# Attention plus eight experts on one core: spilled expert weights leave in six pieces over five tiles and come back one piece at a time

## Reference, cut down

```python
x = x + tanh(g_xattn[0]) * xattn(ctx_1024, layernorm(x), mask, ...)   # 32 batches, 8 heads
h = layernorm(x)                                                      # 3584 tokens of 256
conf = sigmoid(h @ conf_w.T + conf_b) * wealth
top_bids, selected = top_k(conf, 2)                                   # 2 of 8 experts per token
...
ffn = (silu(h @ gate_w.T) * (h @ up_w.T)) @ down_w.T                  # 256 -> 1024 -> 256
out = x + tanh(g_ffn[0]) * sum over the two chosen experts, weighted by softmax(top_bids)
```

## Time and profile before

| | |
|---|---|
| median of 3 runs | 1436.77 us (1435.43 to 1438.32) |
| the profiled execution's own time | 1435.85 us |
| its span, first to last instruction | 1434.3 us |
| mean granted TensorE clock | 0.989 |
| busy: PE, PEld, DVE, ACT, POOL | 94%, 68%, 71%, 65%, 34% |
| bytes moved by DMA | 109.26 MB, mean 76 GB/s |

### The profile page before, as it was taken

One profiled execution on the slowest core, in us unless ns is written; L12 is line 12 of the kernel. 1 busy time (PEld: TensorE's weight loads), 2 busy tenths in 40 slices (PEclk: granted clock), 3 DMA queues, 4 the chain that ended last, 5 costly groups with the idle time before them and its releaser, 6 DMA issues.

```text
span 1434.3 us, 41525 instructions
## 1 busy us (share of the span) xinstructions
PE 1351.1 (94%) x13880; PEld 969.2 (68%) x13880; DVE 1023.5 (71%) x2528; ACT 934.8 (65%) x1932; POOL 488.2 (34%) x659
## 2 busy tenths in 40 slices
PE   2999999999999999999999979999999999999996
PEld 1466666666666666666665657688878778887784
DVE  4688888888888888888888776566556654444442
ACT  5687878787787878878787765566656663333331
POOL 4423322433433334334333143433344333222221
PEclk9999999999999999999999979999999999999998
DMA  4010101111111111111112146433376753112461
GB/s 119 27 42 26 42 23 29 52 40 49 34 53 30 41 46 39 49 33 53 31 33 96 41 129 196 107 98 93 98 211 178 228 152 94 31 31 35 120 203 16
DMA packets 56913, 109.26 MB, mean 76 GB/s; under 512 B 10832, under 2 KB 34768, under 8 KB 56720
## 3 DMA queue, kind: packets, MB, share of 16 engines
q0 software_dynamic: 23712, 55.71, 15.2%
q1 hardware_dynamic: 32160, 49.86, 11.2%
q10 hardware_dynamic: 848, 1.07, 0.3%
HBM read 69.16 MB, written 37.45 MB: 74 GB/s over the span
## 4 chain that ended last, share of the span: by engine, by line
PE 70%; DVE 10%; ACT 6%; issue 6%; DMA 5%; SPq 1%; POOL 1%; POOLq 0%; DVEq 0%; ACTq 0%
PE fP L1542 19%; PE yP L1542 10%; PE uP L1542 10%; PE gP L1542 10%; PE simP L1590 5%; PE ptP L1600 4%; PE tP L1542 3%; PE oP L1542 3%; DVE ms L1036 3%; DVE pT L1042 2%; DMA out<-ysb,xt 2%; PE aP L1773 2%; DVE ao L1054 1%; ACT z L732 1%; PE fP L1558 1%
## 5 line engine op out<-in xcount | busy, mean ns | idle before, releaser
L1542 PE MATMUL fP<-zTs,ws 128*128 128x112 f16 (+1 forms) x1536 | 220.3, 294 | 8.7 <-DVE zTs L1378 5.3
L1542 PE MATMUL fP<-ws,zTs 128*128 128x512 f16 x768 | 186.8, 379 | 0.5 <-DVE kT L1026 0.2
L1036 DVE CUSTOM_DVE_ANT_0 ms<-simP,madd,sim_undo 112x488 f32<-112x488 f32 x256 | 183.9, 720 | 3.3 <-PE simP L1590 1.3
L769 ACT ACTIVATE pr<-ms,nmax 112x488 f32<-112x488 f32 x256 | 179.0, 699 | 3.3 <-DVE nmax L1036 0.5
L1042 DVE SCALAR_TENSOR_TENSOR pT<-ptP,pT 122x448 f16<-122x448 f32 x256 | 157.8, 616 | 28.0 <-ACT pT L776 27.3
L1542 PEld LDWEIGHTS fP<-zTs,ws 128*128 128x128 f16 x1536 | 109.8, 99 | 99.7 <-issue 34.9
L1542 PE MATMUL yP<-W,aT 128*128 (+1 forms) x1512 | 175.4, 273 | 1.8 <-DVE aT L1414 1.8
L1542 PEld LDWEIGHTS yP<-W,aT 128*128 128x128 f16 x1512 | 147.6, 98 | 32.8 <-issue 2.5
L1408 DVE SCALAR_TENSOR_TENSOR act_h<-uP,consts,sg 128x512 f32<-128x512 f32 x126 | 94.5, 750 | 103.1 <-ACT sg L899 102.7
L776 ACT ACTIVATE pT<-ptP 122x448 f16<-122x448 f32 x256 | 137.8, 538 | 40.8 <-PE ptP L1600 39.7
L899 ACT ACTIVATE sg<-gP,consts 128x512 f32<-128x512 f32 x126 | 86.5, 686 | 114.6 <-PE uP L1542 114.4
(11 more groups left out here) (233 smaller groups left out, 2496.2 us busy)
## 6 DMA issues: line engine op xcount, KB each, us to landing
raw<-wffn POOLq DMA_DIRECT2D x36, 512.0 KB, 6.9
split_experts<-W POOLq DMA_DIRECT2D x12, 1024.0 KB, 10.0
W<-split_experts SPq DMA_DIRECT2D x16, 768.0 KB, 7.9
xc<-ctxt SPq DMA_DIRECT2D x32, 375.0 KB
xt<-routed_rows POOLq DMA_DIRECT2D x63, 129.0 KB, 2.4
raw<-wffn SPq DMA_DIRECT2D x12, 512.0 KB, 9.5
routed_rows<-padrows SPq DMA_DIRECT2D x8, 645.0 KB, 7.9
xl<-x SPq DMA_DIRECT2D x32, 112.0 KB
```

The lines of the kernel that those rows point to most:

```text
L769: nc.scalar.activation(pr[h % 2][:, :], ms[h % 2][:, :], ACT.Exp, bias=nmax[p][:, h:h + 1], scale=-1.0, accum_out=rsum[p][:, h:h + 1]).the ...
L1036: nc.vector.tensor_tensor_reduce(out=ms[h % 2][:, :], in0=simP[h % 2][0:S, 0:NK], in1=madd[p][:, :], scale=sim_undo[0:S, 0:1], scalar=3.0e ...
L1542: last = nc.tensor.matmul(o, lhs(k, a), rhs(k, c), start=n == 0, stop=n == len(todo) - 1)
```

## The change

Six edits; no computation changes.

1. Puts: six transfers of 512 KB for a place instead of three of 1024 KB, at steps with t % 5 equal to 0 (one), 1 (one), 2 (two) and 3 (two), each with a semaphore of its own. The loads of `raw` stay where they are.
2. ScalarE's `expert_hi` waits for the put of the same piece only, not for all puts of the place before.
3. Reloads: in `load_place` the wait moves into the loop, behind each of the four transfers.
4. Step 4: `tile_T(5)` on TensorE, and `tile_hi(5)`, `tile_lo(5)` with it, move behind the second half of gate and up.
5. `expert_sums` (TensorE) and `expert_bound` (VectorE) of places 2 to 7 move behind the second half of the same step.
6. Tail: `norm2_T(B - 1)` moves behind the whole second half of tile 0.

```diff
-PUTS = 3
+PUT_AT = {0: (0,), 1: (1,), 2: (2, 3), 3: (4, 5)}
...
                 for c in range(RELOADS):
                     sp.dma_start(W2[:, n % SLOTS, :, c * step_:(c + 1) * step_],
                                  wsp[n - SLOTS, :, :, c * step_:(c + 1) * step_]).then_inc(s_there, 16)
-                sp.wait_ge(s_there, 16 * RELOADS * (n + 1))
+                    sp.wait_ge(s_there, 16 * (RELOADS * n + c + 1))
...
-                sp.wait_ge(s_wput, 16 * PUTS * (n - SLOTS + 1))
+                for c in range(PIECES):
+                    sp.wait_ge(s_wput[c], 16 * (n - SLOTS + 1))
...
-            def put_pieces(p, some):
-
-                cols = slice(some[0] * PCOL, (some[-1] + 1) * PCOL)
-                pool.wait_ge(s_wlo, p * PIECES + some[-1] + 1)
-                pool.dma_start(wsp[p - SLOTS, :, :, cols], W2[:, SLOTS, :, cols]).then_inc(s_wput, 16)
+            def put_piece(p, c):
+
+                pool.wait_ge(s_wlo, p * PIECES + c + 1)
+                pool.dma_start(wsp[p - SLOTS, :, :, piece_cols(c)], W2[:, SLOTS, :, piece_cols(c)]).then_inc(s_wput[c], 16)
...
-                    if done >= SLOTS:
-                        put_pieces(done, FREE_AT[j])
+                if j in PUT_AT and SLOTS <= p - 1 < E:
+                    for c in PUT_AT[j]:
+                        put_piece(p - 1, c)
...
-                    if p > SLOTS:
-                        act.wait_ge(s_wput, 16 * PUTS * (p - SLOTS))
+                if p > SLOTS:
+                    act.wait_ge(s_wput[c], 16 * (p - SLOTS))
...
                 gate_up(0, 0, 0, 0, (1,))
-                gate_up(0, 0, 1, 0, (0,))
+                gate_up(0, 0, 1, 0)
                 norm2_T(B - 1, (B - 1) % 4)
-                gate_up(0, 0, 1, 0, (1,))
                 confidences(B - 1)
...
-                if t == AHEAD - 1:
-                    tile_T(t + 1, (t + 1) % XT_BUFS)
-                if SPAN < t and t // SPAN + 1 < E and t % SPAN == 3:
-                    expert_sums(t // SPAN + 1, bP)
                 if t == 1:
...
                     gate_up(t, q, 1, byte)
+                if t == AHEAD - 1:
+                    tile_T(t + 1, (t + 1) % XT_BUFS)
+                if SPAN < t and t // SPAN + 1 < E and t % SPAN == 3:
+                    expert_sums(t // SPAN + 1, bP)
```

More of the change, by code:

```diff
@@ L298, in build @@
         s_esq, s_bnd, s_ech, s_epow, s_esc = sem("s_esq"), sem("s_bnd"), sem("s_ech"), sem("s_epow"), sem("s_esc")
-        s_whi, s_wlo, s_wput, s_there = sem("s_whi"), sem("s_wlo"), sem("s_wput"), sem("s_there")
+        s_whi, s_wlo, s_there = sem("s_whi"), sem("s_wlo"), sem("s_there")
+        s_wput = [sem(f"s_wput{i}") for i in range(PIECES)]
         s_order, s_padr, s_tab, s_tabch, s_padw = [sem(n) for n in ("s_order", "s_padr", "s_tab", "s_tabch", "s_padw")]
@@ L928, in step @@
                     silu(t, 0, place)
-                if t == AHEAD - 1:
-                    tile_hi(t + 1, 1 - q)
                 if t < NT:
@@ L934, in step @@
                     silu(t, 1, place)
+                    if t == AHEAD - 1:
+                        tile_hi(t + 1, 1 - q)
                     if 0 in TURNED:
@@ L1436, in step @@
                     gated(t, 0, place)
-                if t == AHEAD - 1:
-                    tile_lo(t + 1, 1 - q)
                 if t < NT and 0 not in TURNED:
@@ L1442, in step @@
                     tile_places()
-                if p < E and j == 3 and p > 1:
-                    expert_bound(p, bP)
                 if t < NT:
                     gated(t, 1, place)
+                    if t == AHEAD - 1:
+                        tile_lo(t + 1, 1 - q)
                     if 0 in TURNED:
@@ L1453, in step @@
                 if p < E and j == 3 and p > 1:
+                    expert_bound(p, bP)
                     expert_scale(p)
```

## The result

The change makes the kernel slower: 1450.05 us (median of 6 runs, 1448.65 to 1452.79) against 1436.19 us (6 runs of the kernel before on the same chip, 1433.34 to 1438.32), a ratio of 1.0099 with a 95% interval of 1.0085 to 1.0113, or +13.9 us. The profiled execution took 1448.65 us, its span is 1446.7 us.

What follows compares the result with a forecast made beforehand. TensorE, busy 94% of the span, was taken as the bound. Terms -2.9 - 3.2 + 0.6 - 0.3 + 14.9 + 2.5 = +11.6 us on 1435.85 gave 1447.5; the median, 0.92 higher, 1448.4 us, range 1441 to 1454.

Steps and rivals of the forecast that it cites:

- Edit 3, +14.9 us: Reloads of places 6 and 7: each piece pays its whole way alone, so place 7 lands at 1414.3, wanted at 1399.36.
- The size of a piece: Time of one lone reload transfer from issue to landing, taken as 4.8 us; rival of 3.9 us a piece had 0.15.
- the 1385.3 us for place 6: Landing of place 6's last piece in the kernel before, read as 1376.1 + 0.6 + 8.6, giving 5.4 us of room.
- Clock behind the wait, +2.5 us: After TensorE idles 12 us at the late reload, its lower clock costs 2.5 us (1.7 to 3.5).
- Edit 4, -2.9 us: Step 4: second-half products fill TensorE's wait for tile 5's rows, gaining 2.9 us (bounds 1.5 and 4.1).
- Edit 6, 0: Attention tail: the norm's wait of 1.98 us mostly goes, but TensorE then waits for tile 5's rows, adding 0.
- edits 1 and 2, -0.3 us: Puts in six pieces: ScalarE's squares wait less for `raw`, and TensorE gains 0.3 us (0 to 1.5).
- Edit 5, -3.2 + 0.6 us: Sums of squares: three waits of 3.2 us are covered; the later scale costs 0.1 us in each of six steps.
- All times ahead shift together: At the late reloads, everything ahead moves by the same time, so the front gains do not reduce the delay.

Runs made afterwards that it cites:

- the two kernels on edit 3: The change with its four reload transfers issued together again, 1438.51 us (1.0012); and the kernel before with only the wait behind each transfer added, 1455.44 us (1.0142).
- the four serial kernels: The change, 1450.05 us; it without the moved sums and bound, 1448.28; it with two reload transfers a place, 1441.76; the kernel before with only serial reloads, 1455.44.
- the ten others: The other profiled kernels of fourteen, the kernel before among them, which issue the four transfers of a reload together; they measured 1432.54 to 1439.58 us.
- the transfers of 1.5 MB: The whole change with a place reloaded in two transfers of 1.5 MB instead of four of 0.75 MB, each still waited for: 1441.76 us, 1.0022 to the kernel before.

## Why the prediction was right, and where not

The forecast was 1448.4 us in a range of 1441 to 1454, the median is 1450.05. Sign, place and mechanism of the loss were right. That the sum came within 2 us is in part luck: sizes that were too favourable at the front, edit 5 above all, met sizes that were too dark at the end, and perhaps a gain in steps 28 to 34 that was not forecast.

- **Edit 3, +14.9 us.** The mechanism is shown by the two kernels on edit 3. The waits are 3.03 and 9.24 us where 2.6 and 10 to 15 were said. From the first issue of place 6 to the transposes of step 61 it took 39.9 us (1370.56 to 1410.50), 25.8 before (1373.59 to 1399.36): a delay of 14.2 us, of which 12.3 are waits and most of the rest the slow products between them. A piece took 4.86 us where 4.8 were taken, the hand-over from landing to issue 0.02 us and not 0.15, and the one from place 6 to place 7 0.93 us and not 1.4: 8 x 4.86 + 6 x 0.02 + 0.93 = 39.9 us against 40.7. The size of a piece was the judgement on which the forecast hung, and it was right. One reading behind it was not: the 1385.3 us for place 6 start from its third issue. The fourth stood at 1376.73, so place 6 landed at 1385.9, its room was 4.8 us and not 5.4, and SyncE needed 0.7 us and not 1.3. The page "DMA: Bandwidth & Descriptors" of the Trainium skill (section "Anatomy of one DMA — SWDGE (gpsimd) path") gives its figures for transfers issued from GpSimd, while these are SyncE's. Its fixed part of about 2.0 us agrees with the estimate of 2.0 us above. Estimates by that page of 3.8 us for 0.75 MB and 5.6 us for 1.5 MB lie below the measured 4.86 and 7.74 us.
- **Clock behind the wait, +2.5 us.** Mis-sized. From the transposes of step 61 to the end it is 36.2 us now and 34.9 before, so 1.3 us; the slow block behind the first wait lies ahead of the second wait and shortens it by as much. Steps 59 to 63 as a whole took 55.5 us in the change and 39.9 before: 15.6 us for reload and clock, predicted 17.4.
- **Edit 4, -2.9 us.** Right: 3.3 us less up to down(4), as worked out from the power and ScalarE's copies, about 0.5 us given back in the next step, and 2.4 us by the medians.
- **Edit 6, 0, and edits 1 and 2, -0.3 us.** Right within what can be measured.
- **Edit 5, -3.2 + 0.6 us.** This is the step that failed. It took three waits of one trace as time to be had. Alone it costs 2.7 us (0.9 to 4.7): the product blocks of at least four steps get slower without any wait, and the waits that go are mostly replaced. Why these blocks slow down is not settled. Something paces TensorE's short products (56 ns apart) two steps behind the moved sums, and in step 6 it does so in the kernel before too (blocks of 1.74 and 1.95 us from 916.82 us); that the supply of instructions runs behind is a guess that no run here tests.
- **All times ahead shift together.** About true for the reload, whose first issue came 3.0 us earlier (1370.56 instead of 1373.59), as did the down product of step 58, but the serial reload has a good side that was missed. In steps 28 to 34, where place 4 is reloaded, the four serial kernels took 62.2 us on the mean (61.5 to 63.6) and the ten others 64.1 (62.5 to 65.2). Transfers that come one by one may disturb the loads and copies of the next place less. With so few kernels, and ranges that overlap, this is likely and not shown.

Put together: +15.6 (steps 59 to 63) - 1.8 (steps 28 to 34, likely and not shown) + 1.3 (edit 5 by the table) - 2.4 (edit 4) = +12.7 us, measured +13.9. One number stays open. Edit 3 alone measured +20 us, of which its last steps explain 16.2 (56.1 against 39.9). Its profiled execution was the fastest of four, at 1452.02 us, which is +15.6 and fits; the other three have no trace.

## What to carry to other kernels

A wait behind each of several transfers costs the fixed part every time: a place of four pieces took 20.3 and 18.7 us instead of 12.3 and 12.5, which is 1.8 us more for each piece of 0.75 MB. Nothing shows of it as long as the reload has room, so look for the one reload that has none. A row of waits is no forecast of what moving work gives: the row itself may vary from kernel to kernel (here 0.2 to 3.2 us), so look at what the engine does next, and test each move alone, since here one move's gain hid another's loss. And where an engine waits for a landing, read the queue of that transfer: a small store issued behind six large loads held the start of the expert half.

## What the runs showed of the hardware

- Blocks of 24 short products take 1.50 us or 1.7 to 2.0 us at a granted clock of 1.00 with no wait in the profile. With edit 5 the slow ones stand in steps 10, 15, 25 and 35 in all six kernels that have it.
- The time from issue to landing of a lone transfer was 4.63 to 5.69 us for 0.75 MB and 6.8 to 8.8 us for 1.5 MB. Four pieces in flight brought a place of 3 MB in 12.3 and 12.5 us, 253 GB/s on the mean with 300 to 420 GB/s in most slices of the row above.
- A transfer has landed for its waiter with the last of sixteen increments of the semaphore: SyncE's next issue stood 0.02 us behind it. In the transfers of 1.5 MB that last increment came up to 2.1 us after the fifteenth.
- After 3.03 us and after 9.24 us without work TensorE's next block of 24 products ran at a granted clock of 0.50 and took 2.77 us both times.
- A store of 112 KB took 11.2 us to land behind six loads of 512 KB, and 14.5 us ahead of them but right behind the eight padding stores. What it was queued behind did not shorten its way; only the earlier issue helped.
